# A selective scan whose B is applied by TensorE as a product with diagonals, with an eighth of the C products moved to ScalarE

## The chip, the core and the metric

The kernel runs on one core of a Trainium2 chip. A core has TensorE (PE, matrix products and transposes, which write only to PSUM), VectorE (DVE), ScalarE (ACT), GpSimd (POOL) and SyncE (SP, which only issues transfers here). Each has its own instruction stream; the streams meet at semaphores. The metric is the time of one execution on the device, in microseconds. The median of the runs shown is 1047.11 us (1046.46 to 1047.38, three runs).

## The reference, cut to what matters

A layer of a language model on 8 x 256 tokens: an embedding (192 wide), a two-way Mamba block, and a mixture of 8 experts with two experts per token. All numbers are float32. The change lies in the selective scan of the Mamba block (inner width 384, 16 states, two directions):

```
def selective_scan(u, delta, A, Bm, Cm):
    def step(h, xs):
        d_t, u_t, B_t, C_t = xs
        dA = jnp.exp(d_t[..., None] * A)
        h = dA * h + (d_t * u_t)[..., None] * B_t[:, None, :]
        y = jnp.einsum('bdn,bn->bd', h, C_t)
        return (h, y)
    ...
def ssm_direction(u, x_proj_w, dt_w, dt_b, A_log, D_skip):
    proj = u @ x_proj_w
    dt = jax.nn.softplus(proj[..., :DT_RANK] @ dt_w + dt_b)
    Bm = proj[..., DT_RANK:DT_RANK + D_STATE]
    Cm = proj[..., DT_RANK + D_STATE:]
    A = -jnp.exp(A_log)
    y = selective_scan(u, dt, A, Bm, Cm)
    return y + u * D_skip
y_f = ssm_direction(u, x_proj_w[0], ...)
y_b = jnp.flip(ssm_direction(u_r, x_proj_w[1], ...), axis=1)
y = merge_w[0] * y_f + merge_w[1] * y_b
```

For each state n the input of the recurrence is dt x u x B (per channel and token, times a number per token), its decay is exp(dt x A), and the output is the sum over n of h x C (again a number per token).

## The kernel before, in words

The kernel runs in stages: embedding, norms and the input product; convolution, projections and softplus; the scan; the output product and the router; then a loop over 39 slots of expert work. The change touches the scan stage, and a few lines of its preparation.

**Tiling of the scan.** The 2048 tokens are cut into four groups g of 512 (GT, 4 tiles of 128 tokens, TG). The 384 channels are three blocks (blk) of 128 partitions. A unit u is one group, one direction d and a pair of states (PAIR = 2), so a group has 16 units (UG) and the stage has 64 (NU). An item i is one unit and one block: 192 items, each a tile of 128 channels by 2 states x 512 tokens = 128 x 1024. Within a group a unit's number is r.

**What happens to an item.** B and C are numbers per token, so they are easy to apply where tokens lie on partitions, while the recurrence needs tokens along the row. So the kernel before does this:

- dt x u is kept transposed (tokens on partitions) in dtu_t, four tiles of 128 x 384 for each direction. ScalarE's scale_x (L1182, its activation at L1192) multiplies it by the B of one state and tile, seven activations of 128 x 384 a unit; VectorE's scale_rest (L829, L837) does the eighth.
- TensorE's x_transposes_of (L1462) turns the result back to channels on partitions, eight 128 x 128 transposes an item, into two of four banks of PSUM (X_BANK, by turns).
- ScalarE's exps (L1195, L1206) makes the decays, six activations of 128 x 510 a unit.
- VectorE's scan (L804, L818) runs the recurrence over the item: decay from SBUF, input from PSUM, result into one of STATES = 4 state buffers.
- GpSimd (L559) multiplies the state by C, which a transfer has broadcast over the partitions (c_bc), in place, 128 x 1024.
- TensorE's add (L1476) transposes the eight 128 x 128 pieces and accumulates them in y_ps, three banks of PSUM with tokens on partitions. skip_term (L1492, L1496) adds u x D with a 128 x 128 float32 product by a diagonal, 12 of them a group.

All transposes go through the helper at L1376: the data is the stationary operand, an identity the moving one, with is_transpose set.

**What sets the order.** Every engine's order is written out. TensorE runs a loop over i: the transposes of item i into the x banks (they wait for the scan of item i-2, s_scan, which frees the banks), then add(i-3) (it waits for GpSimd's product, s_mul). At certain units it also transposes a tile of the next group's dt x u (dtu_transposes) into a bank of its own (T_BANK); VectorE copies it out (keep_dtu_t, L844), and GpSimd makes that product (times_u, L548) at r = 4 and r = 9. ScalarE alternates exps(u) and scale_x(u+1). At the end of a group VectorE copies y_ps out (keep_y, L823) before TensorE may start on the next group's sum, and takes the moments of y (moments_y, L635 and L638).

## Time and profile before

| | |
|---|---|
| Median of the runs shown | 1047.11 us (1046.46 to 1047.38) |
| Profiled execution | 1040.84 us, of which the span 1039.1 us |
| Busy, share of the span | PE 74%, DVE 71%, ACT 68%, POOL 62% |
| Scan stage, first to last item | about 185 to 668 us of the span |
| Granted TensorE clock | 0.89 of full speed over the span |

The page of the profile tells busy time, idle time and what ended it for each group of instructions; the timeline lists merged runs of equal instructions in order of time. A busy share over the whole span mixes stages: the scan stage takes 46% of it, and what limits it must be read inside it. PE stands for products and transposes, PEld for loads of the stationary operand. In the profile one float32 product that is no transpose appears as two LDWEIGHTS and two MATMUL, a transpose as one of each.

### The profile page before, as it was taken

The page shows a single profiled execution, that of the slowest core. Times are in us where ns is not written, and L with a number is a line of the kernel's source. Part 1 is how long each engine was busy: PE and PEld are TensorE (multiplying, and loading weights), DVE is VectorE, ACT ScalarE, POOL GpSimd, SP SyncE. Part 2 cuts the span into 40 slices and gives each one's busy share as a digit, 9 for nine tenths or more (in the row PEclk, how much of TensorE's full clock was granted, in tenths as well). Part 3 has the DMA queues.
Part 4 walks back from the last instruction along what each step waited for, and adds up shares of the span by engine and source line. Part 5 has one row for each costly group of instructions (what it writes and reads, how often), then busy time and mean ns, then how long its engine had stood idle before and what let it go on. Part 6 is the DMA issues. An engine that isn't in the chain of part 4 may idle for free. (4 is left out here: it accounts for less than half of the span.)

```text
span 1039.1 us, 14980 instructions
## 1 busy us (share of the span) xinstructions
PE 764.9 (74%) x5308; PEld 665.1 (64%) x5309; DVE 737.8 (71%) x836; ACT 708.7 (68%) x1189; POOL 649.2 (62%) x359
## 2 busy tenths in 40 slices
PE   0559772787878778789887888656626887999991
PEld 0225321677777777678776877556525877999991
DVE  4898387899999999999999999964155111222224
ACT  0134895999999999899998999324242444565652
POOL 7435555699998999799998999602113656221120
PEclk9969665899999999999999999986655899899996
DMA  4012101112123112212111222299986752000005
GB/s 85 0 61 121 66 26 28 55 61 82 62 81 123 61 65 79 82 62 76 68 62 70 73 82 81 78 314 211 258 188 149 144 129 60 24 19 23 19 23 190
DMA packets 31902, 91.92 MB, mean 88 GB/s; under 512 B 7560, under 2 KB 15264, under 8 KB 30824
## 3 DMA queue, kind: packets, MB, share of 16 engines
q1 hardware_dynamic: 20792, 57.53, 16.4%
q0 software_dynamic: 8352, 27.07, 12.1%
q10 hardware_dynamic: 2704, 6.61, 1.9%
q8 instruction: 32, 0.52, 0.2%
q14 instruction: 22, 0.18, 0.1%
HBM read 77.67 MB, written 13.53 MB: 88 GB/s over the span
## 5 line engine op out<-in xcount | busy, mean ns | idle before, releaser
L1376 PE MATMUL ps<-ident,arena 128*128 128x128 f32 (+1 forms) x3390 | 433.3, 282 | 171.6 <-DVE arena L818 54.7
L1376 PEld LDWEIGHTS ps<-ident,arena 128*128 128x128 f32 (+1 forms) x3390 | 381.0, 144 | 218.4 <-DVE arena L818 70.2
L559 POOL TENSOR_TENSOR arena<-arena 128x1024 f32<-128x1024 f32 x192 | 426.7, 2248 | 44.0 <-DVE arena L818 41.6
L818 DVE TENSOR_TENSOR_SCAN arena<-arena,ps 128x1024 f32<-128x1024 f32 x192 | 428.0, 2271 | 5.0 <-PE ps L1376 3.6
L1206 ACT ACTIVATE arena<-arena,neg_a 128x510 f32<-128x510 f32 x384 | 241.4, 714 | 0.0
L1192 ACT ACTIVATE arena<-arena 128x384 f32<-128x384 f32 x224 | 116.8, 607 | 9.0 <-PE ps L1376 8.9
L1192 ACT ACTIVATE arena<-ln_in,arena 128x384 f32<-128x384 f32 x224 | 116.8, 609 | 5.5 <-PE ps L1376 5.4
L1035 DVE TENSOR_SCALAR ln_in<-ps 128x768 f32<-128x768 f32 x39 | 37.3, 957 | 112.4 <-PE ps L1619 82.0
L618 POOL DMA_INDIRECT y_rows<-arena x39 | 37.9, 971 | 115.1 <-DVE arena L1040 107.6
L1629 PE MATMUL ps<-arena,ln_in 128*128 x468 | 85.4, 332 | 9.8 <-issue 7.2
L1629 PEld LDWEIGHTS ps<-arena,ln_in 128*128 128x128 f32 x468 | 76.9, 194 | 10.5 <-issue 10.4
L1619 PE MATMUL ps<-arena,ln_in 96*128 96x128 f32 x456 | 59.2, 290 | 6.6 <-issue 6.6
L1619 PEld LDWEIGHTS ps<-arena,ln_in 96*128 96x128 f32 x456 | 58.2, 205 | 8.6 <-issue 8.6
L1327 ACT ACTIVATE arena<-ps 96x256 f32<-96x256 f32 x39 | 14.7, 378 | 71.0 <-PE ps L1376 47.7
L1619 PE MATMUL ps<-arena 96*128 96x128 f32 x480 | 59.0, 280 | 1.9 <-issue 1.3
L1619 PEld LDWEIGHTS ps<-arena 96*128 96x128 f32 x480 | 58.0, 196 | 2.6 <-issue 2.5
L1040 DVE COPY arena<-ps 128x192 f32 (+1 forms) x39 | 13.9, 357 | 60.5 <-PE ps L1629 44.6
L543 POOL TENSOR_TENSOR arena<-arena 128x1536 f32<-128x1536 f32 x8 | 37.6, 4698 | 29.1 <-DVE arena L773 29.1
L582 POOL DMA_INDIRECT arena<-x_rows,arena x39 | 37.4, 959 | 27.2 <-issue 16.5
L563 POOL DMA_DIRECT2D arena<-wf x8 | 7.5, 943 | 71.0 <-ACT arena L1273 68.7
L1339 ACT ACTIVATE ln_in<-ln_in 128x768 f32<-128x768 f32 x39 | 32.8, 842 | 20.4 <-DVE ln_in L1035 19.2
L538 POOL TENSOR_TENSOR arena<-arena 128x1536 f32<-128x1536 f32 x8 | 27.3, 3432 | 22.0 <-ACT arena L1126 22.0
(206 smaller groups left out, 830.0 us busy)
## 6 DMA issues: line engine op xcount, KB each, us to landing
arena<-b_rows SPq DMA_DIRECT2D x64, 512.0 KB, 3.5
arena<-ws SPq DMA_DIRECT2D x16, 576.0 KB, 9.3
arena<-wf POOLq DMA_DIRECT2D x16, 576.0 KB
arena<-hf POOLq DMA_DIRECT2D x16, 576.0 KB
gates_dram<-arena SPq DMA_DIRECT2D x4, 1536.0 KB, 5.1
arena<-gates_dram ACTq DMA_DIRECT2D x3, 1536.0 KB, 12.9
arena<-y_rows SPq DMA_DIRECT2D x4, 768.0 KB, 7.2
arena<-gates_dram SPq DMA_DIRECT2D x1, 1536.0 KB, 8.8
```

The source lines that it names most:

```text
L543: g_.tensor_tensor(sp_pos[n % SP], sp_pos[n % SP], sp_w[n % SP], ALU.subtract).then_inc(s_rc, 1)
L559: g_.tensor_tensor(state[i % STATES], state[i % STATES], c_bc[u % C_BUFS], ALU.mult).then_inc(s_mul, 1)
L582: g_.indirect_dma_start(out=slot_rows[:, s, :], out_offset=None, in_=x_rows, in_offset=bass.IndirectOffsetOnAxis(ap=src_row[:, s:s + 1].bi ...
L618: g_.indirect_dma_start(out=y_rows, out_offset=bass.IndirectOffsetOnAxis(ap=dst_row[:, s:s + 1].bitcast(U32), axis=0), in_=slot_rows[:, s, ...
L818: v.tensor_tensor_scan(o, a, x, 0.0, ALU.mult, ALU.add).then_inc(s_scan, 1)
L1035: v.tensor_scalar(h_t[half].rearrange("p (a b) c -> p a (b c)", a=2), ps[:, bank:bank + 2, 0:HH], 0.0, None, ALU.max).then_inc(s_hr, 1)
L1192: last = a.activation(xt(u % 2, n, t), dtu_t[g % 2][d][:, t, :].rearrange("p (b c) -> p b c", b=DB), ACT.Copy, scale=bt[:, TG * g + t, col ...
L1206: last = a.activation(out_a[:, n, :, lo:hi], src[:, :, lo:hi], ACT.Exp, scale=neg_a[:, blk, d, PAIR * pair + n:PAIR * pair + n + 1])
L1339: a.activation(h_t[half], h_t[half], ACT.Square).then_inc(s_h, 1)
L1376: return mm(o, src, ident[at:at + parts, at:at + parts], start=start, stop=True, is_transpose=True, skip_group_check=True)
L1619: last = mm(ps[:, H_BANKS[half] + j // 3, P * (j % 3):P * (j % 3) + P], w1_cur[half][0:KC + k, k, P * j:P * j + P], slot_x_t[half][0:KC + ...
L1629: last = mm(ps[:, 3, 0:C], h_t[half][:, j, :], w2_all[:, bass.ds(e * (HB * C) + j * C, C)], start=j == 0, stop=j == HB - 1)
```

## The change

**B as a diagonal.** ScalarE no longer scales dt x u. Its b_diagonals makes, for each state and token tile of a unit, a 128 x 128 diagonal from the identity with B on it: eight activations of 128 x 128 a unit. TensorE's x_products_of multiplies: dtu_t (tokens on partitions) is the stationary operand, the diagonal the moving one, and the product is the scaled input, already with channels on partitions. It is an ordinary float32 product, not a transpose: eight an item. VectorE's scale_rest is gone.

**The last piece of C.** In 15 of a group's 16 units (has_last) GpSimd multiplies 896 of 1024 columns. The last piece of a unit, second state and fourth token tile, is transposed unmultiplied, for its three blocks, into T_BANK (last_transposes); ScalarE copies it out times C (last_times_c, 128 x 384), and TensorE adds it to y_ps by a product with the identity (last_sum, 128 x 384). The transposes that add makes of this piece go away in turn. bt holds C beside B for it, so its transposes and copies before the stage are twice as wide.

**Order and buffers.** There are six state buffers in place of four, and VectorE's wait for them is by whole units. ScalarE's exps(u) is split in two calls with last_times_c(u-2) between. times_u for the second direction comes at the last block of r = 8, keep_dtu_t and dtu_transposes one item run and one unit earlier.

TensorE's stream in the scan stage, one unit of before (from an item with a group's dtu_transposes on), with the semaphores waited for:

```order
L1376 MATMUL ps<-ident,arena 128x128 [waits scan_done,x_t_scaled_by_vector,x_t_scaled_by_scalar]
L1376 MATMUL ps<-ident,arena 128x128 x7
L1376 MATMUL ps<-ident,arena 128x128 [waits c_multiplied]
L1376 MATMUL ps<-ident,arena 128x128 x7
L1376 MATMUL ps<-ident,arena 128x128 [waits scan_done]
L1376 MATMUL ps<-ident,arena 128x128 x7
L1376 MATMUL ps<-ident,arena 128x128 [waits c_multiplied]
L1376 MATMUL ps<-ident,arena 128x128 x7
L1376 MATMUL ps<-ident,arena 128x128 [waits dtu_t_ready,dtu_product_ready]
L1376 MATMUL ps<-ident,arena 128x128 x2
```

And one unit of the change at the same place (L1379 is the transpose helper, L1477 the products by diagonals, L1516 last_sum):

```order
L1477 MATMUL ps<-arena,ln_in 128x128 [waits scan_done,dtu_t_ready,b_diagonals_ready]
L1477 MATMUL ps<-arena,ln_in 128x128 x7
L1379 MATMUL ps<-ident,arena 128x128 [waits c_multiplied]
L1379 MATMUL ps<-ident,arena 128x128 x6
L1477 MATMUL ps<-arena,ln_in 128x128 [waits scan_done]
L1477 MATMUL ps<-arena,ln_in 128x128 x7
L1379 MATMUL ps<-ident,arena 128x128 [waits c_multiplied]
L1379 MATMUL ps<-ident,arena 128x128 x6
L1516 MATMUL ps<-arena,ident 128x384 [waits last_piece_times_c]
L1379 MATMUL ps<-ident,arena 128x128 [waits dtu_t_ready,dtu_product_ready]
L1379 MATMUL ps<-ident,arena 128x128 x2
L1379 MATMUL ps<-ident,arena 128x128 [waits dtu_t_ready,last_piece_times_c,c_multiplied]
```

The eight transposes ahead of each scan became eight products; seven transposes stand where eight stood behind c_multiplied, the last item of a unit has three more (into T_BANK), and one 128 x 384 product a unit is new. dtu_transposes moved from behind the third item of a unit to behind the second.

ScalarE's stream, a unit of before:

```order
L1192 ACTIVATE arena<-ln_in,arena 128x384 [waits x_in_banks,dtu_t_ready]
L1192 ACTIVATE arena<-ln_in,arena 128x384 x6
L1206 ACTIVATE arena<-arena,neg_a 128x2x255 [waits scan_done]
L1206 ACTIVATE arena<-arena,neg_a 128x2x255
L1206 ACTIVATE arena<-arena,neg_a 128x2x255 [waits scan_done]
```

and of the change:

```order
L1180 ACTIVATE arena<-ident,arena 128x128 [waits x_in_banks]
L1180 ACTIVATE arena<-ident,arena 128x128 x7
L1194 ACTIVATE arena<-arena,neg_a 128x2x255 [waits scan_done]
L1194 ACTIVATE arena<-arena,neg_a 128x2x255
L1194 ACTIVATE arena<-arena,neg_a 128x2x255 [waits scan_done]
L1194 ACTIVATE arena<-arena,neg_a 128x2x255
L1206 ACTIVATE arena<-ps,arena 128x384 [waits last_piece_transposed]
```

Seven wide activations became eight narrow ones, and a copy out of PSUM came in before the last two decays.

The diff, cut to its core:

```diff
@@ -34,7 +34,7 @@
 HT = TILES // 2
-STATES, C_BUFS = 4, 3
+STATES, C_BUFS = 6, 3
 SP = 3
...
@@ -159,22 +160,17 @@
         dt_all = [[cut([DB, GT]) for _ in range(2)] for _ in range(NG)]
-        bt = cut([TILES, 2 * NS])
+        bt = cut([TILES, 4 * NS])
         fronts = used[0]
...
         state = [cut([PAIR, GT]) for _ in range(STATES)]
-        ODD = P + 1
-        xt_flat = [cut([PAIR * TG * DI + DB * (ODD - P)]) for _ in range(2)]
+        b_diag = [cut([PAIR, TG, P]) for _ in range(2)]
+        h_tok = [cut([DI]) for _ in range(2)]
         dtu_t = [[ln_flat[:, TG * DI * d:TG * DI * (d + 1)].rearrange("p (t c) -> p t c", t=TG) for d in range(2)],
                  [cut([TG, DI]) for _ in range(2)]]
-        def xt(i, n, t, blk=None):
-
-            at, step = DI * (TG * n + t), ODD if (n, t) == (PAIR - 1, TG - 1) else P
-            if blk is not None:
-                return xt_flat[i][:, at + step * blk:at + step * blk + P]
-            return xt_flat[i][:, at:at + DB * step].rearrange("p (b c) -> p b c", b=DB)[:, :, 0:P]
+        used[0] = max(used[0], DTU_AT)
         dtu = cut([DB, GT])
...
@@ -412,6 +410,12 @@
+        def has_last(u):
+            return u % UG != UG - 1
+
+        def last_of(u):
+            return u - u // UG
+
         def alone(eng):
...
@@ -550,13 +554,15 @@
                 g, r = divmod(u, UG)
-                if blk == 0 and r in (4, 9) and g + 1 < NG:
-                    times_u(g + 1, r // 9)
+                if (r, blk) in ((4, 0), (8, DB - 1)) and g + 1 < NG:
+                    times_u(g + 1, r // 8)
                 if blk == 0:
...
                 pool.wait_ge(s_scan, i + 1)
-                g_.tensor_tensor(state[i % STATES], state[i % STATES], c_bc[u % C_BUFS], ALU.mult).then_inc(s_mul, 1)
+                n = PAIR * GT - (P if has_last(u) else 0)
+                h = state[i % STATES].rearrange("p n t -> p (n t)")[:, 0:n]
+                g_.tensor_tensor(h, h, c_bc[u % C_BUFS].rearrange("p n t -> p (n t)")[:, 0:n], ALU.mult).then_inc(s_mul, 1)
...
@@ -809,7 +815,7 @@
-                    dve.wait_ge(s_sum, i - STATES + 1)
+                    dve.wait_ge(s_sum, DB * ((i - STATES) // DB + 1))
                 a = decay[d][blk].rearrange("p n t -> p (n t)")
...
@@ -826,35 +832,18 @@
-            def scale_rest(u):
-
-                g, pair, d = unit_of(u)
-                n = NS * d + PAIR * pair + PAIR - 1
-                dve.wait_ge(s_dtu_t, 8 * g + TG * (d + 1))
-                if u >= 2:
-
-                    dve.wait_ge(s_x_ps, DB * (u - 1))
-                v.tensor_scalar(xt(u % 2, PAIR - 1, TG - 1), dtu_t[g % 2][d][:, TG - 1, :].rearrange("p (b c) -> p b c", b=DB),
-                                bt[:, TG * g + TG - 1, n:n + 1], None, ALU.mult).then_inc(s_xt_v, 1)
-
             def keep_dtu_t(g, d, t):
...
-            dve.wait_ge(s_dtu_t, 2 * TG)
-            dve.wait_ge(s_bt, NG)
-            scale_rest(0)
-            scale_rest(1)
             for g in range(NG):
...
                         scan(IG * g + DB * r + blk)
-                        if blk == 1 and g + 1 < NG and 6 <= r < 6 + 2 * TG:
-                            keep_dtu_t(g + 1, *divmod(r - 6, TG))
-                        if blk == DB - 1 and UG * g + r + 2 < NU:
-                            scale_rest(UG * g + r + 2)
+                        if blk == 1 and g + 1 < NG and 5 <= r < 5 + 2 * TG:
+                            keep_dtu_t(g + 1, *divmod(r - 5, TG))
                         if g and r == 0 and blk == 1:
...
@@ -1137,7 +1126,7 @@
                 act.wait_ge(s_bt_ps, g + 1)
-                a.activation(bt[:, TG * g:TG * (g + 1), :], ps[:, 1, 0:TG * 2 * NS].rearrange("p (t n) -> p t n", t=TG), ACT.Copy).then_inc(s_bt, 1)
+                a.activation(bt[:, TG * g:TG * (g + 1), :], ps[:, 1, 0:TG * 4 * NS].rearrange("p (t n) -> p t n", t=TG), ACT.Copy).then_inc(s_bt, 1)
...
@@ -1179,24 +1168,23 @@
-            def scale_x(u):
+            def b_diagonals(u):
                 g, pair, d = unit_of(u)
-                act.wait_ge(s_dtu_t, 8 * g + TG * (d + 1))
                 if u >= 2:
...
                     act.wait_ge(s_x_ps, DB * (u - 1))
-                for k in range(PAIR * TG - 1):
-                    n, t = divmod(k, TG)
+                for n in range(PAIR):
                     col = NS * d + PAIR * pair + n
-                    last = a.activation(xt(u % 2, n, t), dtu_t[g % 2][d][:, t, :].rearrange("p (b c) -> p b c", b=DB), ACT.Copy, scale=bt[:, TG * g + t, col:col + 1])
-                last.then_inc(s_xt_a, 1)
-
-            def exps(u):
+                    for t in range(TG):
+                        last = a.activation(b_diag[u % 2][:, n, t, :], ident[:], ACT.Copy, scale=bt[:, TG * g + t, col:col + 1])
+                last.then_inc(s_b_diag, 1)
+
+            def exps(u, blks):
...
                 lo, hi = (1, SEQ) if d == 0 else (0, SEQ - 1)
-                for blk in range(DB):
+                for blk in blks:
                     if u >= 2:
...
@@ -1206,6 +1194,16 @@
                     last.then_inc(s_decay, 1)
+
+            def last_times_c(u):
+
+                g, pair, d = unit_of(u)
+                act.wait_ge(s_last_ps, last_of(u) + 1)
+                if last_of(u) >= 2:
+
+                    act.wait_ge(s_last_sum, last_of(u) - 1)
+                col = 2 * NS + NS * d + PAIR * pair + PAIR - 1
+                a.activation(h_tok[last_of(u) % 2], ps[:, T_BANK, 0:DI], ACT.Copy, scale=bt[:, TG * g + TG - 1, col:col + 1]).then_inc(s_last, 1)
...
@@ -1220,17 +1218,22 @@
             act.wait_ge(s_bt, NG)
-            scale_x(0)
+            b_diagonals(0)
             keep_first_dtu_t(1)
...
                 g, r = divmod(u, UG)
-                exps(u)
+                exps(u, range(DB - 1))
+                if u >= 2 and has_last(u - 2):
+                    last_times_c(u - 2)
+                exps(u, (DB - 1,))
                 if u + 1 < NU:
-                    scale_x(u + 1)
+                    b_diagonals(u + 1)
                 if u == UG * (NG - 1) + 4:
...
+
+            last_times_c(NU - 2)
...
@@ -1459,18 +1462,20 @@
-            def x_transposes_of(i):
+            def x_products_of(i):
                 u, blk = divmod(i, DB)
+                g, _, d = unit_of(u)
                 if blk == 0:
-                    pe.wait_ge(s_xt_a, u + 1)
-                    pe.wait_ge(s_xt_v, u + 1)
+                    pe.wait_ge(s_b_diag, u + 1)
+                    pe.wait_ge(s_dtu_t, 8 * g + TG * (d + 1))
                 if i >= 2:
...
                     for t in range(TG):
-                        last = transpose(ps[:, X_BANK + PAIR * (i % 2) + n, P * t:P * t + P], xt(u % 2, n, t, blk), P)
+                        last = mm(ps[:, X_BANK + PAIR * (i % 2) + n, P * t:P * t + P], dtu_t[g % 2][d][:, t, P * blk:P * blk + P],
+                                  b_diag[u % 2][:, n, t, :], start=True, stop=True)
                 last.then_inc(s_x_ps, 1)
...
@@ -1481,13 +1486,34 @@
                     pe.wait_ge(s_yv, g)
+                if has_last(i // DB) and blk == DB - 1:
+                    last_transposes(i // DB)
                 for n in range(PAIR):
                     for t in range(TG):
+                        if has_last(i // DB) and (n, t) == (PAIR - 1, TG - 1):
+                            continue
                         c = t * DB + blk
...
                 last.then_inc(s_sum, 1)
+
+            def last_transposes(u):
+
+                g, r = divmod(u, UG)
+                if last_of(u):
+                    pe.wait_ge(s_last, last_of(u))
+
+                pe.wait_ge(s_dtu_t, 8 * NG if g + 1 == NG else 8 * (g + 1) + min(max(r - 3, 0), 2 * TG))
+                for b in range(DB):
+                    last = transpose(ps[:, T_BANK, P * b:P * b + P], state[(DB * u + b) % STATES][:, PAIR - 1, GT - P:GT], P)
+                last.then_inc(s_last_ps, 1)
+
+            def last_sum(u):
+
+                pe.wait_ge(s_last, last_of(u) + 1)
+                c = (TG - 1) * DI
+                mm(y_ps[:, c:c + DI], ident[:], h_tok[last_of(u) % 2], start=False, stop=True, skip_group_check=True).then_inc(s_last_sum, 1)
...
@@ -1505,13 +1531,18 @@
                 if i < ITEMS:
-                    x_transposes_of(i)
+                    x_products_of(i)
                 if i >= LAG:
                     add(i - LAG)
+                    u, blk = divmod(i - LAG, DB)
+                    if blk == 1 and u and has_last(u - 1):
+                        last_sum(u - 1)
                 if i < ITEMS and i % DB == DB - 1:
...
                         skip_term(g, r - 2)
+                if i < ITEMS and i % DB == 1:
+                    g, r = divmod(i // DB, UG)
                     if g + 1 < NG and 5 <= r < 5 + 2 * TG:
```

## Rows read from the trace of the kernel before

**Rows 1.** Stage windows: busy time (instructions) of each engine, granted clock, DMA share, GB/s
```profile
186.00:302.00 116.00, 95.89 (x782) 87.12 (x781) 113.63 (x70) 116.00 (x210) 108.09 (x48) 0.97 0.19 65
302.00:423.00 121.00, 97.68 (x807) 88.77 (x805) 119.44 (x82) 116.09 (x209) 111.80 (x50) 0.99 0.23 83
423.00:539.00 116.00, 94.04 (x783) 84.75 (x784) 115.29 (x78) 110.31 (x199) 108.24 (x48) 1.00 0.21 73
539.00:650.00 111.00, 92.17 (x753) 82.90 (x752) 110.97 (x71) 107.07 (x195) 101.63 (x47) 0.98 0.20 73
```

**Rows 2.** Line groups, 270 to 700 us: busy us, mean ns, idle before by releaser
```profile
L559 POOL TENSOR_TENSOR arena<-arena 128x1024 f32<-128x1024 f32 x160 | 355.9, 2250 | 28.0 <-DVE arena L818 25.9 <-issue 0.3
L818 DVE TENSOR_TENSOR_SCAN arena<-arena,ps 128x1024 f32<-128x1024 f32 x159 | 354.2, 2270 | 2.2 <-PE ps L1376 1.5 <-issue 0.5
L1376 PE MATMUL ps<-ident,arena 128*128 128x128 f32 x2628 | 324.4, 278 | 87.4 <-DVE arena L818 48.8 <-POOL arena L559 12.5 <-DVE arena L875 7.4
L1376 PEld LDWEIGHTS ps<-ident,arena 128*128 128x128 f32 x2628 | 289.7, 143 | 120.0 <-DVE arena L818 61.8 <-issue 23.1 <-POOL arena L559 17.4
```

**Rows 3.** Timeline, one unit: start us, us, engine, line, count, idle before
```profile
647.88 3.79 ACT L1206 ACTIVATE arena<-arena,neg_a 128x510 f32<-128x510 f32 x6
649.43 1.94 PE L1376 MATMUL ps<-ident,arena 128*128 128x128 f32 x16 [0.30 <-DVE arena L818]
...
651.37 0.59 DVE L837 TENSOR_SCALAR arena<-arena 128x384 f32<-128x384 f32 x1
...
651.55 3.66 ACT L1192 ACTIVATE arena<-arena 128x384 f32<-128x384 f32 x7
651.88 13.16 DVE L818 TENSOR_TENSOR_SCAN arena<-arena,ps 128x1024 f32<-128x1024 f32 x6
```

**Rows 4.** Timeline around one run of skip_term's products
```profile
205.95 0.75 PEld L1496 LDWEIGHTS ps<-skip,arena 128*128 128x128 f32 x6
206.06 0.83 PE L1496 MATMUL ps<-skip,arena 128*128 128x128 f32 x6
206.62 1.78 PEld L1376 LDWEIGHTS ps<-ident,arena 128*128 128x128 f32 x16
```

**Rows 5.** Line L1496: durations ns min/median/max, first and last start
```profile
L1496 PE MATMUL ps<-skip,arena x96: 275/275/275, 206.1 to 593.1; 128*128 128x128 f32 x96
```

**Rows 6.** Timeline and line L1408: float32 products of 384 columns, back to back
```profile
74.70 5.33 PE L1408 MATMUL ps<-arena 96*128 96x384 f32 x16
...
L1408 PE MATMUL ps<-arena x64: 484/486/1009, 46.9 to 101.7; 96*128 96x384 f32 x64
```

**Rows 7.** Timeline, the first boundary between groups
```profile
309.84 1.74 DVE L823 COPY arena<-ps 128x1536 f32<-128x1536 f32 x1
...
314.18 1.93 DVE L635 BATCH_NORM_STATS2 stats<-arena 128x6 f32<-128x384 f32 x4
316.15 0.38 DVE L638 BATCH_NORM_AGGREGATE mv<-stats 128x2 f32<-128x6 f32 x4
316.45 6.61 DVE L818 TENSOR_TENSOR_SCAN arena<-arena,ps 128x1024 f32<-128x1024 f32 x3
318.75 3.47 PEld L1376 LDWEIGHTS ps<-ident,arena 128*128 128x128 f32 x22 [3.20 <-DVE arena L818]
```

**Rows 8.** Timeline, start of the stage
```profile
182.70 1.64 ACT L1180 ACTIVATE ln_in<-ps 128x384 f32<-128x384 f32 x4 [0.33 <-PE ps L1376]
...
185.19 1.94 PE L1376 MATMUL ps<-ident,arena 128*128 128x128 f32 x16 [2.53 <-DVE arena L837]
```

**Rows 9.** Timeline, the last transposes of the stage
```profile
667.25 1.09 PE L1376 MATMUL ps<-ident,arena 128*128 128x128 f32 x8 [0.86 <-POOL arena L559]
```

**Rows 10.** Lines L1140, L844, L548: durations ns min/median/max
```profile
L1140 ACT ACTIVATE arena<-ps x4: 258/259/277, 116.3 to 159.1; 128x128 f32<-128x128 f32 x4
...
L844 DVE COPY arena<-ps x16: 531/535/540, 235.6 to 531.9; 128x384 f32<-128x384 f32 x16
...
L548 POOL TENSOR_TENSOR arena<-arena x6: 3458/3462/3472, 217.7 to 499.3; 128x1536 f32<-128x1536 f32 x6
```

More of the change, by code:

```diff
@@ L50 @@
 GATE_W = 2 * TG * DI
+DTU_AT = 38336
 class Steps:
@@ L344, in build @@
         s_ln_y = sem("y_norm_variance_ready")
-        s_xt_a = sem("x_t_scaled_by_scalar")
-        s_xt_v = sem("x_t_scaled_by_vector")
+        s_b_diag = sem("b_diagonals_ready")
+        s_last_ps = sem("last_piece_transposed")
+        s_last = sem("last_piece_times_c")
+        s_last_sum = sem("last_piece_summed")
         s_x_ps = sem("x_in_banks")
@@ L1443, in _ @@
                 for t in range(TG):
-                    last = transpose(ps[:, 1, 2 * NS * t:2 * NS * (t + 1)], lb[g % 2][64:96, P * t:P * t + P], 2 * NS, at=64)
+                    last = transpose(ps[:, 1, 4 * NS * t:4 * NS * (t + 1)], lb[g % 2][64:128, P * t:P * t + P], 4 * NS, at=64)
                 last.then_inc(s_bt_ps, 1)
```

## The prediction

> **What bounds the kernel now.** I read the windows of the scan stage first, then the groups of lines, then the timeline of one unit. In four stretches that cover nearly all of the stage VectorE is busy 459.3 of 464 us, while TensorE shows 379.8, ScalarE 449.5 and GpSimd 429.8 [rows 1]. The groups say the same from the side of the waits: the scans have stood idle 2.2 us in all, while the transposes waited 48.8 us for scans [rows 2]. So VectorE's scan of an item is what everything else waits for. The timeline shows the period of a unit [rows 3]: the small multiplication of scale_rest at 651.37, the next scans at 651.88, three of them taking 13.16/6 x 3 = 6.58 us; with the 0.51 us that scale_rest holds the engine a unit is 7.09 us.
>
> TensorE has room in that unit, and the question is how much. It runs sixteen transposes for an item in 1.94 us [rows 3] of the item's 2.36 us. A run of 16 loads of the stationary operand takes 1.78 us, each 143 ns long [rows 2, 4]; they start (1.78 - 0.143)/15 = 0.109 us apart. That spacing, not the 278 ns that one lasts, is what a transpose costs when the engine is full: 48 a unit is 5.2 us of 7.09. Some 1.9 us a unit is free.
>
> **The change part by part.**
>
> *The products by diagonals.* They have an exact likeness before: skip_term, a 128 x 128 float32 product with a diagonal as the moving operand. Three such products stand in the profile as six loads and six MATMULs, and the loads of the next run begin 206.62 - 205.95 = 0.67 us after theirs [rows 4], so one of the pair costs 0.112 us and a product 0.223 us. All 96 of them last 275 ns [rows 5], the same everywhere in the stage. A transpose costs 0.109 us. The eight of an item go from 0.87 to 1.79 us. Whole stage: 192 x 8 = 1536 products x 0.223 = 343 us, for 167 us of transposes. This is the large term, and it falls on the engine that had 1.9 us free a unit: 24 x (0.223 - 0.109) = 2.7 us is more than that.
>
> The Trainium skill speaks against this edit in "Perfetto Trace Analysis", section Optimizing Tensor Performance: logical transposes should use the transpose mode, as opposed to a standard matmul. "TensorE: Matmul & The Clock Gate", section Terms, says that the transpose mode is 4 times faster for float32. The direction agrees with this trace, the factor doesn't: here it is 0.223/0.109 = 2.05. By the page's factor the sum would be larger, and it stands below as a rival; mine goes by the row.
>
> *The last piece.* The transposes of states stay at 24 a unit (three less in the sum, three more into the separate bank): 1536 x 0.109 = 167 us. last_sum is new: 60 products of 384 columns. Sixteen MATMULs of that width, back to back, took 5.33 us, the last 0.486 us of it its own length, so they start (5.33 - 0.486)/15 = 0.323 us apart [rows 6]; two a product make 0.646 us, and 60 of them 39 us. skip_term stays at 48 x 0.223 = 11 us, the transposes of dt x u at 72 x 0.109 = 8 us. TensorE's work in the stage is 343 + 167 + 39 + 11 + 8 = 568 us, or 8.9 us a unit, against VectorE's 6.58 (its 0.51 us of scale_rest is gone). TensorE becomes the bound.
>
> *Who hides now.* VectorE has 2.3 us to spare a unit. GpSimd: 896 of 1024 columns at 2.25 us [rows 2] is 2.0 us an item, 5.9 us a unit. ScalarE before: 3.79 + 3.66 us [rows 3]. Now 3.79 us of decays, eight activations of 128 x 128 at no more than 0.26 us [rows 10], and one copy of 384 columns out of PSUM, bounded by 0.41 us (1.64/4 [rows 8]) and 0.52 us (3.66/7 for the wide ones that go [rows 3]): 6.4 us of 8.9. It is off the path too, as are the doubled copies of bt. What all these edits save is therefore worth nothing.
>
> *The waits.* TensorE meets them in its own order, and behind a waiting instruction stands all of its stream. Products of item i wait for scan i-2: after the products of i-2 come seven transposes (0.76), the products of i-1 (1.79) and seven to ten more (0.9), 3.5 us against 2.27 for the scan. The sum of item i-3 waits for GpSimd's product, 2.27 + 2.25 us after the x banks are full, against some 8 us. last_transposes waits for VectorE's copy of dt x u, whose transposes ran just one item before: scan 2.27 + copy 0.54 [rows 10] = 2.8 us after the x banks were filled, against 0.76 + 0.65 + 0.33 + 1.79 = 3.5 us on TensorE. This is the tightest, 0.7 us, 24 times. times_u (3.46 us [rows 10]) at the end of r = 8 comes 2.3 + 2.0 + 3.5 = 7.8 us after x(25) was filled, and TensorE asks for it after 10. last_times_c comes back a unit before it is needed. I cost them at nothing; uncovered, 1 us at each of the 24 places is 24 us.
>
> *The three boundaries between groups.* There TensorE waits even if it is the bound: VectorE copies y_ps (1.74), runs a scan (2.2), the moments (1.93 + 0.38) and the next scan (2.2) [rows 7], with the two x banks empty in turn. From the last sum of a group at 0: copy to 1.9, scan of the third item to 4.1, moments to 6.3, fourth item to 8.5. TensorE fills x at 1.8, waits 0.1, sums, stands from 2.9 to 4.1, works to 6.8, stands to 8.6. That is 3.1 us each, 9 us in all. Bounds: 0, and twice that.
>
> *Start, clock and end.* The first products wait for the last copies of dt x u, 182.70 + 1.64 = 184.3 us [rows 8], so they start at 184.5; before it was 185.19. Filling the pipeline costs 1 us. The granted clock was 0.97, 0.99, 1.00 and 0.98 of full speed [rows 1]; the shares that these leave open, times the stretches, are 7 us of lost speed, at 1.2 in place of 2.4 GHz. TensorE stood for 3.2 us at a boundary [rows 7] and will stand for less. I take 3 us, between 0 and 7. At the end a last scan and product of the full width stand open, 0.9 us more than TensorE's own work.
>
> *The sum.* 568 + 9 + 1 + 3 + 1 = 582 us from 184.5, an end of the stage at 766.5. Before, the last transposes ended at 667.25 + 1.09 = 668.3 [rows 9]. Nothing behind the stage is touched, and all of it starts when the last sum is done. So +98 us on the profiled execution of 1040.84, 1139 us, and on the median of 1047.11, which lies 6 us above that execution, 1145 us.
>
> **The rivals.**
>
> *VectorE stays the bound (the other side).* If a product cost less than it does in skip_term, since so many stand in a row, TensorE could stay under 6.58 us a unit. It would need a MATMUL every (6.58 - 2.62 - 0.61 - 0.29)/48 = 0.064 us (24 transposes, last_sum and the small ones taken off) where 0.112 was seen. Then 64 x 0.51 = 33 us are saved: 1014 us. For it: VectorE's 99% busy share, and no long run of such products in the stage to look at. Against it: the 0.112 us of six in a row, and the transposes ahead of and behind them, which run at their own pace without a gap.
>
> *The waits bite.* TensorE is the bound and its covered waits aren't covered: the copy behind the tightest wait, boundaries at twice the price, the low clock at 7 us: 24 + 9 + 4 = 37 us more at the worst, 20 to 37 likely, some 1170 us. For it: the 0.7 us of slack. Against: scans of 2.27 us that vary by some hundredths.
>
> *A product costs four transposes.* By the factor of 4 of "TensorE: Matmul & The Clock Gate" in the Trainium skill, it would be so. From the rows, 4 x 0.109 = 0.436 us a product is 1536 x 0.213 = 327 us more than my sum: 1472 us. The row of skip_term has it at half of this, so 1 in 100.
>
> **How the numbers follow.** My forecast 0.84, the waits 0.11, VectorE as the bound 0.04, four transposes 0.01. The likeliest is 1145 us. Its own range: 14 us of boundaries, start, clock and end gone is 1131; 20 us of waits is 1165. With the second rival the range reaches up to 1172, and down to 1130. A change of 0.2% is about what can be told from none, 1045.0 to 1049.2 us; only a mixture of the first case and the other side could fall there, 0.01. Faster 0.04, slower 0.95.
>
> **What would show it.** The groups of the changed kernel must have 3072 MATMULs for the products by diagonals, not 1536. In a stage window TensorE should be without idle time and VectorE at 75 to 80% busy; the scans should have waited for the products, and the products for nearly nobody. The unit's period in the timeline should be 8.6 to 9.2 us, and ScalarE's diagonals should last 0.26 us or less. The prediction is wrong if the loads of the products start less than 0.1 us apart, if TensorE shows waits of over 0.5 us in each unit, or if the stage ends outside 750 to 795 us.

## The result and the profile after

The changed kernel takes 1142.74 us (median of four runs, 1139.63 to 1144.33); beside it the kernel before took 1046.78 us (1043.98 to 1047.38, four runs). The ratio is 1.0919, 95% interval 1.0888 to 1.095: slower by 96 us. The forecast was 1145 us.

The profiled execution took 1144.33 us, span 1142.6 us. First the same stage windows as [rows 1], here for the changed kernel: stretch, its length, busy time (instructions) of PE, PEld, DVE, ACT and POOL, granted clock, DMA share, GB/s.

```profile
184.00:300.00 116.00, 114.83 (x967) 111.39 (x968) 90.31 (x46) 86.98 (x198) 84.41 (x40) 0.97 0.16 55
300.00:440.00 140.00, 137.10 (x1179) 132.41 (x1179) 111.58 (x63) 99.93 (x227) 103.45 (x48) 1.00 0.20 69
440.00:580.00 140.00, 137.10 (x1179) 132.42 (x1179) 111.78 (x63) 101.04 (x234) 103.69 (x48) 1.00 0.17 58
580.00:720.00 140.00, 137.10 (x1175) 132.40 (x1175) 110.61 (x59) 101.17 (x230) 98.15 (x48) 1.00 0.18 61
```

The four lines cover 184 to 720 us of the stage. TensorE is busy in 526.1 of these 536 us; VectorE, full before, is down to 424.3 of 536, or 79%. The stage runs from 184.42 us to 768.84 us, 584.4 us where it had 483.2. The groups of lines in the stage, of the changed kernel, say who waits for whom; they answer to [rows 2].

```profile
L824 DVE TENSOR_TENSOR_SCAN arena<-arena,ps 128x1024 f32<-128x1024 f32 x192 | 438.6, 2286 | 119.4 <-PE ps L1477 100.0 <-issue 19.0 <-ACT arena L1194 0.3
L565 POOL TENSOR_TENSOR arena<-arena 128x896 f32<-128x896 f32 x192 | 404.8, 2111 | 166.6 <-DVE arena L824 166.0
L1379 PE MATMUL ps<-ident,arena 128*128 128x128 f32 x1608 | 210.6, 273 | 1.8 <-POOL arena L565 1.4 <-DVE arena L829 0.5
L1477 PE MATMUL ps<-arena,ln_in 128*128 128x128 f32 x1536 | 189.9, 278 | 5.5 <-DVE arena L824 3.5 <-ACT ln_in L1169 2.0
L1477 PE MATMUL ps<-arena 128*128 128x128 f32 x1536 | 187.6, 275 | 5.5 <-DVE arena L824 5.5
```

The direction of waiting has turned. Before, the scans stood idle 2.2 us between 270 and 700 us, and the transposes waited for scans. Now the scans wait 100 us for the products of L1477, and the products wait for scans 9 us in the whole stage (3.5 and 5.5 us in the two lines of L1477). The 1536 products stand as 2 x 1536 MATMULs.

One unit in the timeline of the changed kernel (start us, us, engine, line, count, idle before), answering to [rows 3, 4]:

```profile
561.02 1.95 PE L1477 MATMUL ps<-arena,ln_in 128*128 128x128 f32 x16
...
562.70 0.80 PEld L1379 LDWEIGHTS ps<-ident,arena 128*128 128x128 f32 x7
562.81 0.93 PE L1379 MATMUL ps<-ident,arena 128*128 128x128 f32 x7
563.06 2.29 DVE L824 TENSOR_TENSOR_SCAN arena<-arena,ps 128x1024 f32<-128x1024 f32 x1 [0.26 <-PE ps L1477]
...
563.57 0.81 PE L1516 MATMUL ps<-arena,ident 128*128 128x384 f32 x2
...
564.54 1.95 PE L1477 MATMUL ps<-arena,ln_in 128*128 128x128 f32 x16
565.26 0.53 DVE L839 COPY arena<-ps 128x384 f32<-128x384 f32 x1
566.22 1.13 PEld L1379 LDWEIGHTS ps<-ident,arena 128*128 128x128 f32 x10
566.33 1.25 PE L1379 MATMUL ps<-ident,arena 128*128 128x128 f32 x10
...
572.02 2.29 DVE L824 TENSOR_TENSOR_SCAN arena<-arena,ps 128x1024 f32<-128x1024 f32 x1 [0.26 <-PE ps L1477]
```

The eight products of an item, sixteen MATMULs, hold TensorE from 561.02 to 562.81, 1.79 us. The scan of an item starts at 563.06 and the scan of the same block one unit later at 572.02: a period of 8.96 us. Between these rows TensorE's MATMULs show no idle time.

The first boundary between groups, same kernel, which answers to [rows 7]:

```profile
336.40 1.76 DVE L829 COPY arena<-ps 128x1536 f32<-128x1536 f32 x1 [1.84 <-PE ps L1379]
338.07 2.28 DVE L824 TENSOR_TENSOR_SCAN arena<-arena,ps 128x1024 f32<-128x1024 f32 x1
338.30 0.96 PE L1379 MATMUL ps<-ident,arena 128*128 128x128 f32 x7 [0.15 <-DVE arena L829]
340.27 1.91 DVE L641 BATCH_NORM_STATS2 stats<-arena 128x6 f32<-128x384 f32 x4
340.40 2.05 PE L1477 MATMUL ps<-arena 128*128 128x128 f32 x16 [1.14 <-DVE arena L824]
342.21 0.38 DVE L644 BATCH_NORM_AGGREGATE mv<-stats 128x2 f32<-128x6 f32 x4
342.51 6.74 DVE L824 TENSOR_TENSOR_SCAN arena<-arena,ps 128x1024 f32<-128x1024 f32 x3
344.82 2.05 PE L1477 MATMUL ps<-arena 128*128 128x128 f32 x16 [1.60 <-DVE arena L824]
```

TensorE stands 0.15, 1.14 and 1.60 us here, 2.9 us a boundary; the other two boundaries show the same within 0.01 us.

### The profile page after: what moved, and what is told of

Same layout as the page of the kernel before. It is cut to its first block, busy times and chain, and to the rows that moved or that the text cites. A ratio compares the mean times of both kernels' runs of the same rounds, so it can differ in the third digit from the quotient of the medians.

```text
span 1142.6 us, 18343 instructions
## 1 busy us (share of the span) xinstructions
PE 948.3 (83%) x6964; PEld 865.9 (76%) x6965; DVE 723.5 (63%) x772; ACT 665.9 (58%) x1313; POOL 627.5 (55%) x359
## 4 chain that ended last, share of the span: by engine, by line
PE 70%; DVE 11%; DMA 6%; ACT 5%; issue 3%; POOL 2%; another core or an unknown queue 1%; ACTq 0%; DVEq 0%; POOLq 0%; SPq 0%
PE ps L1477 30%; PE ps L1379 16%; PE ps L1650 9%; PE ps L1660 7%; PE ps L1516 3%; DMA x_rows<-arena 2%; DVE arena L824 2%; DMA arena<-gates_dram 1%; PE ps L1574 1%; DMA arena<-wf 1%; PE ps L1522 1%; PE ps L1439 1%; ACT arena L1276 1%; DMA arena<-hf 1%
## 5 line engine op out<-in xcount | busy, mean ns | idle before, releaser
L565 POOL TENSOR_TENSOR arena<-arena 128x896 f32<-128x896 f32 x192 | 404.8, 2111 | 166.6 <-DVE arena L824 166.0
L1379 PE MATMUL ps<-ident,arena 128*128 128x128 f32 (+2 forms) x1854 | 257.7, 281 | 81.5 <-DVE arena L710 34.3
L1379 PEld LDWEIGHTS ps<-ident,arena 128*128 128x128 f32 (+2 forms) x1854 | 218.4, 144 | 100.9 <-issue 46.2
L1477 PE MATMUL ps<-arena,ln_in 128*128 128x128 f32 x1536 | 189.9, 278 | 5.5 <-DVE arena L824 3.5
L1477 PE MATMUL ps<-arena 128*128 128x128 f32 x1536 | 187.6, 275 | 5.5 <-DVE arena L824 5.5
L1477 PEld LDWEIGHTS ps<-arena,ln_in 128*128 128x128 f32 x1536 | 182.6, 194 | 10.0 <-issue 3.3
L1477 PEld LDWEIGHTS ps<-arena 128*128 128x128 f32 x1536 | 180.8, 192 | 12.3 <-DVE arena L824 6.4
L1180 ACT ACTIVATE arena<-ident,arena 128x128 f32<-128x128 f32 x512 | 156.2, 393 | 2.1 <-PE ps L1477 2.1
L1206 ACT ACTIVATE arena<-ps,arena 128x384 f32<-128x384 f32 x60 | 34.9, 582 | 159.8 <-PE ps L1379 159.8
L1660 PEld LDWEIGHTS ps<-arena,ln_in 128*128 128x128 f32 x468 | 79.9, 200 | 10.3 <-issue 10.3
L547 POOL TENSOR_TENSOR arena<-arena 128x1536 f32<-128x1536 f32 x8 | 37.6, 4701 | 29.2 <-DVE arena L779 29.2
```

Of the source, the lines that this page charges most:

```text
L547: g_.tensor_tensor(sp_pos[n % SP], sp_pos[n % SP], sp_w[n % SP], ALU.subtract).then_inc(s_rc, 1)
L565: g_.tensor_tensor(h, h, c_bc[u % C_BUFS].rearrange("p n t -> p (n t)")[:, 0:n], ALU.mult).then_inc(s_mul, 1)
L1180: last = a.activation(b_diag[u % 2][:, n, t, :], ident[:], ACT.Copy, scale=bt[:, TG * g + t, col:col + 1])
L1206: a.activation(h_tok[last_of(u) % 2], ps[:, T_BANK, 0:DI], ACT.Copy, scale=bt[:, TG * g + TG - 1, col:col + 1]).then_inc(s_last, 1)
L1379: return mm(o, src, ident[at:at + parts, at:at + parts], start=start, stop=True, is_transpose=True, skip_group_check=True)
L1477: last = mm(ps[:, X_BANK + PAIR * (i % 2) + n, P * t:P * t + P], dtu_t[g % 2][d][:, t, P * blk:P * blk + P], b_diag[u % 2][:, n, t, :], st ...
```

## The experiments

They ran on three other chips, on which everything behind the scan stage takes some 350 us, not 371 to 374. The kernel before took 1021.93 us on the one with the first four edits of the changed kernel, 1022.29 us on the one with the changed kernel again and the first three mixtures, and 1023.53 us on the one with the last two mixtures. So ratios to the kernel before on the same chip and lengths of the stage are compared. Differences in us between the first four edits and the changed kernel are between two chips, on which the kernel before differs by 0.4 us.

**The changed kernel again.** No edit.

> The changed kernel unchanged, timed beside the others on their chip. The scan stage takes 584 us as in the first trace, the ratio to the kernel before is 1.09 to 1.10 whatever the rest of the kernel takes on this chip.

Measured: 1120.76 us, ratio 1.0947 (1.0922 to 1.0971), stage 582.2 us. The ratio is as on the first chip (1.0919, 1.0888 to 1.095), and the loss lies in the stage. Differences below are to 1120.76 us and 582.2 us.

**Products at the price of transposes.**

```diff
-                        last = mm(ps[:, X_BANK + PAIR * (i % 2) + n, P * t:P * t + P], dtu_t[g % 2][d][:, t, P * blk:P * blk + P],
-                                  b_diag[u % 2][:, n, t, :], start=True, stop=True)
+                        last = transpose(ps[:, X_BANK + PAIR * (i % 2) + n, P * t:P * t + P], dtu_t[g % 2][d][:, t, P * blk:P * blk + P], P)
```

> The changed kernel with one edit: the 1536 products by diagonals are issued as transposes (identity as the moving operand), so B is left out of the computation; ScalarE still makes the diagonals. If the price of the products on TensorE is the whole cause, TensorE needs 584 - 1536 x (0.223 - 0.109) = 409 us for the stage, the scans become the bound again (192 x 2.2 us, the copies and the boundaries, about 450 us), and the time is about 1010 us (1000 to 1025): below the kernel before. Rival, the new waits or the order (six state buffers, last piece, later times_u) cost the time: it stays above 1080 us.

Measured: 998.49 us, ratio 0.9772 (0.9751 to 0.9794); stage 460.4 us. That is 122 us below the changed kernel, where about 133 (118 to 143) were expected. The ratios give 120 us. With the same waits, buffers and order, the way in which the 1536 products are issued makes all of the loss and more. (The edit leaves B out of the result.) The group of the scans in this run, 200 to 640 us:

```profile
L824 DVE TENSOR_TENSOR_SCAN arena<-arena,ps 128x1024 f32<-128x1024 f32 x187 | 413.2, 2267 | 9.4 <-PE ps L1379 5.7 <-ACT arena L1194 1.9 <-issue 1.8
```

Their idle time is 9.4 us, where it is 82.7 us in the same stretch of the changed kernel: VectorE is the bound again. The run also shows what the rest of the change was worth, 23 us, had the products cost nothing more.

**Diagonals alone.**

```diff
         def has_last(u):
-            return u % UG != UG - 1
+            return False
...
-            last_times_c(NU - 2)
```

> The changed kernel without the last piece: GpSimd multiplies all 1024 columns in every unit, no last_transposes, last_times_c and last_sum. If TensorE's work sets the stage, its 60 products of 384 columns go (60 x 0.646 = 39 us) and the time is about 1104 us (1098 to 1110). Rival, last_sum hides or was worth something to GpSimd: 1143 us or more. Rival, the waits around the last piece cost beside its work: below 1095 us.

Measured: 1082.72 us, ratio 1.0591 (1.0574 to 1.0607). That is 38.0 us less than the changed kernel (39 expected); the ratios give 36 us. The stage is 546.7 us, 35.5 us less. The two stages differ in one more thing: this one ran at half speed, the lower clock, for 5.8 us at its start and 1.6 us at its end, and the other never (granted 0.99 and 1.00 over the stage). With half of these 7.4 us taken off, the difference of the stages is 39 us by estimate. So the last piece cost TensorE's time for its 60 products of 384 columns, and nothing beyond it that these runs could tell. What it took from GpSimd was worth nothing here.

**Longer copies behind the tightest wait.**

```diff
+                for _ in range(2):
+                    st.then(v.tensor_copy(spare_t[:], ps[:, T_BANK, 0:DI]))
                 v.tensor_copy(dtu_t[g % 2][d][:, t, :], ps[:, T_BANK, 0:DI]).then_inc(s_dtu_t, 1)
```

> The changed kernel, with each of the 24 copies of keep_dtu_t preceded by two more copies of the same 128 x 384 into a spare tile, about 2 x 0.6 us of VectorE that last_transposes waits for. My theory, that this wait was covered by 0.4 us in the trace after: (1.2 - 0.4) x 24 = 19 us, 1162 us (1155 to 1168). Rival, VectorE's idle 2.3 us a unit absorbs it: 1143 us. Rival, no cover at all: 29 us, 1172 us.

Measured: 1140.87 us, ratio 1.115 (1.1127 to 1.1172); 20.1 us more than the changed kernel, 19 expected; the stage is 603.2 us, 21 us more. The timeline of this run:

```profile
562.62 1.12 DVE L841 COPY spare_t<-ps 128x384 f32<-128x384 f32 x2
563.78 0.56 DVE L842 COPY arena<-ps 128x384 f32<-128x384 f32 x1
...
564.45 1.07 PEld L1382 LDWEIGHTS ps<-ident,arena 128*128 128x128 f32 x10 [0.79 <-issue]
564.48 1.28 PE L1382 MATMUL ps<-ident,arena 128*128 128x128 f32 x10 [0.63 <-DVE arena L842]
```

The last copy ends at 564.34 us. A single one of 0.53 us, begun at 562.62 like these, would have ended 1.2 us earlier. TensorE's load waits 0.79 us, so 0.4 us were cover. The wait exists, it was hidden, and it had less room than the 0.7 us that I had worked out.

**Moments spread over four units.**

```diff
-                        if g and r == 0 and blk == 2:
-                            moments_y(g - 1)
+                        if g and 2 <= r < 2 + TG and blk == 2:
+                            if r == 2:
+                                dve.wait_ge(s_yv, g)
+                            st(v.bn_stats(stats[:, TG * (g - 1) + r - 2, :], y_all[g - 1][:, r - 2, :]))
+                        if g and r == 2 + TG and blk == 2:
+                            ...
-                if u == UG * (NG - 1) + 4:
+                if u == UG * (NG - 1) + 10:
```

> The changed kernel, with the moments of y taken one tile at a time behind the third scan of r = 2 to 5 (and their four aggregations behind that of r = 6) in place of all at the group's boundary; the rsqrt that needs them comes six units later on ScalarE. My theory of the boundary says that TensorE's second stand of 1.87 us there comes from the moments and goes, the first of 1.4 us from the copy of y and stays: 3 x 1.8 = 5 us less, 1138 us. Rival, the stand comes from the scans alone: no change, 1143 us.

Measured: 1114.5 us, ratio 1.0917 (1.0898 to 1.0935); 6.3 us less than the changed kernel (5 expected), but the intervals of the two ratios overlap, so the times alone don't show it. The stage is 576.6 us, 5.6 us less. The timeline at this run's first boundary:

```profile
335.39 1.76 DVE L829 COPY arena<-ps 128x1536 f32<-128x1536 f32 x1 [1.84 <-PE ps L1386]
337.07 6.76 DVE L824 TENSOR_TENSOR_SCAN arena<-arena,ps 128x1024 f32<-128x1024 f32 x3
337.30 0.95 PE L1386 MATMUL ps<-ident,arena 128*128 128x128 f32 x7 [0.15 <-DVE arena L829]
339.40 2.05 PE L1484 MATMUL ps<-arena 128*128 128x128 f32 x16 [1.15 <-DVE arena L824]
...
342.05 1.95 PE L1484 MATMUL ps<-arena 128*128 128x128 f32 x16
```

The first stand (1.15 us) is there, the second (1.60 us) is gone, and so it is at the other two boundaries: the products wait for scans 4.3 us in this stage and 9.1 us in that of the changed kernel timed again, 4.8 us or 3 x 1.60 less. The moments made the second stand.

**A mixture: four pieces by diagonals, four as before.** TensorE's free time in the kernel before is enough for some of the products. The kernel before, without scale_rest, with ND of a unit's eight pieces by diagonals:

```diff
-        ODD = P + 1
-        xt_flat = [cut([PAIR * TG * DI + DB * (ODD - P)]) for _ in range(2)]
+        NW = PAIR * TG - ND
+        xt_wide = [cut([NW, DI]) for _ in range(2)]
+        b_diag = [cut([ND, P]) for _ in range(2)]
...
+                    if k < NW:
+                        last = a.activation(xt_wide[u % 2][:, k, :], dtu_t[g % 2][d][:, t, :], ACT.Copy, scale=bt[:, TG * g + t, col:col + 1])
+                    else:
+                        last = a.activation(b_diag[u % 2][:, k - NW, :], ident[:], ACT.Copy, scale=bt[:, TG * g + t, col:col + 1])
...
+                        if k < NW:
+                            last = transpose(o, xt_wide[u % 2][:, k, P * blk:P * blk + P], P)
+                        else:
+                            last = mm(o, dtu_t[g % 2][d][:, t, P * blk:P * blk + P], b_diag[u % 2][:, k - NW, :], start=True, stop=True)
```

> The kernel before with only part of the change: of a unit's eight pieces of input four go by diagonals and products, four by wide activations and transposes as before; scale_rest is gone; no last piece, four state buffers. If each engine's work a unit decides, TensorE has 5.2 + 12 x 0.114 + 0.3 = 6.9 us, ScalarE 7.1 + 0.52 - 4 x 0.21 = 6.8 us, VectorE 6.6 us, GpSimd 6.75 us and twice 3.46 us a group; the stage takes 455 to 468 us in place of 483, the ratio to the kernel before is 0.978 (0.972 to 0.988). Rival, four engines this close to each other wait in turn and nothing comes of it: ratio 0.99 to 1.01.

Measured: 1022.4 us, ratio 0.9994 (0.9978 to 1.0011), stage 485.5 us, where a ratio of 0.978 and a stage of 455 to 468 us were expected. My expectation fell. Three windows of this run:

```profile
210.00:300.00 90.00, 86.78 (x771) 84.94 (x770) 84.19 (x45) 87.45 (x180) 90.00 (x39) 1.00 0.21 71
330.00:420.00 90.00, 86.67 (x771) 84.94 (x770) 83.75 (x45) 84.01 (x170) 90.00 (x38) 1.00 0.24 87
450.00:540.00 90.00, 87.14 (x777) 85.48 (x776) 83.93 (x45) 83.66 (x170) 89.75 (x38) 1.00 0.20 70
```

GpSimd is full. I had priced its multiplication at the 2.25 us of [rows 2]; here it takes 2387 ns on the mean, so three are 7.2 us, no less than the 7.09 us of a unit before. TensorE is at 97% in these windows. In the chain of work that ended last, 200 to 640 us, GpSimd has 44% and TensorE 43%, so what the waits among nearly full engines, the rival, add wasn't separated.

The mean of [rows 2] hid two durations. First the kernel before, then this run (shortest, median and longest in ns):

```profile
L559 POOL TENSOR_TENSOR arena<-arena x192: 1987/2370/2411, 188.8 to 665.2; 128x1024 f32<-128x1024 f32 x192
L556 POOL TENSOR_TENSOR arena<-arena x192: 2336/2379/2463, 191.5 to 668.5; 128x1024 f32<-128x1024 f32 x192
```

In the kernel before, the 66 multiplications of the units whose C lies in c_bc[0], the first of three buffers, took 1.99 to 2.03 us, and the 126 others 2.35 to 2.41 us. In this run all 192 take 2.34 us or more. What sets c_bc[0] apart is its place. In the kernel before it begins 6 words past a multiple of 16 words of the arena, because of the odd spacing in xt_flat; in the changed kernel and all mixtures, from which xt_flat is gone, it begins at a multiple of 16, as the other two always do. So with the new layout 66 x 0.38 = 25 us of GpSimd's time came on, a side effect of the edit. In the changed kernel that is hidden, since GpSimd waits there; in the mixture it falls on a full engine. No run moves this buffer alone: that its place is the cause, and what the mixture would take with the old place, isn't shown.

**The same with three diagonals.** ND = 3.

> Three pieces by diagonals, five as before, the rest as in the mixture with four. TensorE has 6.55 us a unit, ScalarE 6.97. By the work of the engines 64 x 0.07 us more than with four: ratio 0.98 (0.975 to 0.99). If TensorE is what limits the mixture it is faster than that with four, if ScalarE, slower by 5 to 15 us.

Measured: 1020.83 us, ratio 0.9981 (0.9967 to 0.9995), stage 484.3 us; 0.98 was expected, so this fell too. It is 1.6 us faster than with four, and the intervals overlap. Less work for TensorE moves little, as one expects with GpSimd full (337.6 of 340 us in four windows).

**The mixture with times_u on VectorE.**

```diff
-                if blk == 0 and r in (4, 9) and g + 1 < NG:
-                    times_u(g + 1, r // 9)
...
+                        if (r, blk) in ((4, 0), (9, 0)) and g + 1 < NG:
+                            times_u(g + 1, r // 9)
```

> The same with times_u (six products of 128 x 1536) moved from GpSimd to VectorE. If GpSimd is the last bound of the mixture this saves up to 20 us of its work for 10 us of VectorE's: stage 450 to 460 us, ratio 0.97. Rival, two engines that read SBUF at once stretch each other (the same kind of product took 1.75 or 4.88 us on VectorE in the trace before): 6 x 3 us more, ratio 0.98 to 0.99.

Measured: 1015.49 us, ratio 0.9915 (0.9889 to 0.994), stage 480.5 us: under 1% faster than the kernel before, with an interval clear of 1, and faster than the changed kernel. The gain is less than half of what the theory of GpSimd as the bound gave (ratio 0.97, stage 450 to 460 us). In four windows of this run VectorE is at 331.8 and GpSimd at 332.5 of 340 us. The rival of this run, that the two engines stretch each other, shows in the durations of GpSimd's multiplications (L554) and of the moved ones on VectorE (L782, two of them ahead of the stage):

```profile
L554 POOL TENSOR_TENSOR arena<-arena x192: 2351/2377/3885, 189.0 to 661.3; 128x1024 f32<-128x1024 f32 x192
L782 DVE TENSOR_TENSOR arena<-arena x8: 1733/1976/4883, 148.8 to 497.1; 128x1536 f32<-128x1536 f32 x8
```

Five of the six moved multiplications took 1.73 to 2.37 us, and GpSimd's beside each took 3.74 to 3.89 us where 2.37 is usual. The sixth took 4.58 us itself, and GpSimd's beside it 2.35. So about 1.5 us were lost five times on GpSimd and 2.6 us once on VectorE.

**The same with the moments spread.** The edit of the moments above, on the mixture.

> The mixture with four diagonals and times_u on VectorE, with the moments of y taken a tile at a time behind r = 2 to 5. At a boundary TensorE stood 0.9, 1.3 and 2.3 us; the last should go, and the low clock around it: 3 x 2 us of the stage, 474 to 476 us, ratio to the kernel before 0.986 (0.980 to 0.990) against 0.9915 for the mixture alone. Rival, VectorE is the bound there, busy 98%, and moving its work gains nothing: ratio 0.990 to 0.993.

Measured: 1015.34 us, ratio 0.9912 (0.9874 to 0.995). The trace shows a stage of 475.4 us, as expected (480.5 us without the edit, on another chip), but the times don't tell it from the mixture without. In four windows VectorE is busy 337.7 of 340 us, which fits the rival. Undecided.

**And with three diagonals.** The same with ND = 3.

> The same with three diagonals. TensorE has 0.34 us less a unit, ScalarE 0.2 us more. In the mixture with four, TensorE and VectorE are the fullest (97 and 98%): if TensorE decides, 3 to 10 us faster than with four; if VectorE or GpSimd, equal within 3 us; if ScalarE, slower.

Measured: 1016.37 us, ratio 0.994 (0.9911 to 0.9969). That is 1.0 us more than with four, within the 3 us expected if VectorE or GpSimd decides, and the intervals overlap. The stage is 481.0 us.

## Why the prediction was right

*TensorE's passes.* The step that carried the forecast was the price of a product, 0.223 us, from six MATMULs of skip_term. Here sixteen take 1.79 us, 0.112 each, also in a full stream. The run with cheap products shows this price to be the cause, and VectorE 79% busy fits. The factor of 4 in "TensorE: Matmul & The Clock Gate" of the Trainium skill (section Terms) doesn't hold for these 128 x 128 pieces: the two prices here are 0.223 and 0.109 us, a factor of 2.05. With 4 the time would have grown by some 425 us.

*The last piece.* Forecast 39 us, measured 38.0 by leaving it out. That it saved nothing through GpSimd fits the waits of the changed kernel: GpSimd waits 166 us for scans there.

*The sum.* Stage 582 us forecast, 584.4 measured; unit 8.9, measured 8.96. The boundaries were forecast with stands of 0.1, 1.2 and 1.8 us and showed 0.15, 1.14 and 1.60; the cause of the last is shown by the spread moments. The start was right within 0.1 us, and filling the pipeline cost TensorE a wait of 0.75 us, forecast 1. The clock was put at 3 us; 5.6 us at the start of the stage ran at half speed, which is 2.8. At the end TensorE waits 1.4 us for GpSimd's last product; 1 was forecast. Under 3 us of the stage stay unexplained.

*Behind the stage.* Nothing was forecast to change. In the profiled executions that part took 373.8 us against 370.7, with TensorE at the low clock for 147 us instead of 129. On the chip on which the changed kernel was timed again it took 350.9 us in the changed kernel and 350.5 and 351.4 us in the mixtures with three and four diagonals, so the 3 us belong to this pair of executions and aren't shown to come from the change. What moved the clock stays open.

*Luck.* The median came out 2.3 us below the forecast, which is closer than the working is. The stage grew by 101.2 us for 98 forecast, and the pair of profiled executions differs by 103.5 us. That the medians differ by only 96.0 us comes from where these executions lie: the one before was 6 us below its median, the one after 1.6 us above its own.

*The range.* The rival of the waits was priced at 37 us at the worst, which is 1182 us, and the range was closed at 1172. Nothing came near it.

*Mis-sized, and off the path.* ScalarE's diagonals were put at 0.26 us or less, from an activation out of PSUM without a scale from memory [rows 10]. They take 0.39 us, so that sign, named in the prediction, came out wrong:

```profile
L1180 ACT ACTIVATE arena<-ident,arena x512: 386/393/415, 178.5 to 749.8; 128x128 f32<-128x128 f32 x171
L1206 ACT ACTIVATE arena<-ps,arena x60: 581/582/584, 200.9 to 763.3; 128x384 f32<-128x384 f32 x60
```

Back to back eight of them take 2.44 us. It cost nothing, since ScalarE had over 2 us a unit to spare (by estimate: 3.8 + 2.4 + 0.6 us of 8.96).

GpSimd's multiplication of 896 columns was put at 2.0 us, a share of the mean of [rows 2]. It took 2.10 us; the same share of 2.38 us, the longer of the two durations in that mean, is 2.08. This cost nothing either.

The cover of the tightest wait was 0.4 us and not 0.7. In the timeline above TensorE takes 3.52 us from its first load behind the products (562.70) to the load that needs the copy (566.22), as forecast (3.5). But the scan starts at 563.06, 0.36 us after 562.70, where I had put nothing, and the copy behind it is done at 565.79, 3.1 us after 562.70 in place of 2.8.

## What to carry to other kernels

Moving scaling into a matrix product isn't free where a transpose was already being paid: count loads and MATMULs of the new form by their spacing in a full run, for one unit of the pipeline, and set that against what the receiving engine has free, which was 1.9 us here against 2.7 us added by the products and 0.6 us by the last piece. In this case work taken from engines behind the new bound was worth nothing. And when the first bound is lifted, look at the second in the same unit, with the shortest, median and longest duration of its instruction and not the mean alone: GpSimd's mean of 2.25 us was made of 2.00 and 2.38 us, the shorter went with one buffer's place, and an edit that had nothing to do with GpSimd moved that buffer.

## What the runs showed of the hardware

- A 128 x 128 float32 product is two loads and two MATMULs 0.112 us apart at full clock, a transpose one of each at 0.109 us; a product of 384 columns has its two 0.323 us apart. A mixed stream runs at the sum of these: 48 x 0.112 + 27 x 0.109 + 0.646 = 8.97 us for the unit whose period is 8.96.
- A scale from memory costs ScalarE time of its own: copies of 128 x 384 out of PSUM into SBUF took 0.49 us without one (the group of four in [rows 8]: 1.64 us back to back) and 0.58 us with one (last_times_c); 128 x 128 took 0.26 us without [rows 10] and, from SBUF, 0.39 us with one. The Trainium skill says this in "ScalarE: Activation LUTs", section What ACT_TABLE_LOAD costs: a fixed part of 186 ns, 0.83 ns a column, and about 93 ns for each operand that is a pointer to a number per partition. An estimate from these figures of the page for 128 columns with one pointer is 0.386 us, and the run agrees with 0.393. I had taken the row without.
- GpSimd's product of 128 x 1024 had two durations in the kernel before: 1.99 to 2.03 us in the 66 whose C lies in c_bc[0], and 2.35 to 2.41 us in the 126 others. Where all three buffers begin at a multiple of 16 words, all took 2.34 us or more. The scan beside it doesn't make the difference: within the kernel before, the shorter and the longer ones stand beside the same scans, and VectorE is 99% busy. No run isolates the buffer's place.
- A product of two tensors in SBUF on VectorE and one on GpSimd that run at once stretch one of the two. In the traces of the three mixtures with times_u on VectorE (18 such products), either VectorE's took 4.51 to 4.99 us and GpSimd's beside it 2.35 to 2.41, or VectorE's took 1.73 to 2.37 us and GpSimd's 3.74 to 3.90.
